# Two of the four value products of the token mixer, their sums and the experts' preparation start in the next loop body

## The reference

```python
x = x + tanh(g_xattn[0]) * attention(layernorm(x), ctx, mask)      # 16 heads of 64, causal
# the token mixer: attention among the 16 heads of one token
h = rmsnorm(layernorm(x), gamma1)
q = (h @ Wq + bq).reshape(b, t, 16, 16)
kv = ((h @ Wdown + bdown) @ Wup + bup)                             # k, v: (b, t, 16, 16)
att = softmax(einsum('bthd,btgd->bthg', q, k) / 4)
o = einsum('bthg,btgd->bthd', att, v)
y = layernorm(x) + o @ Wo + bo
# eight experts, all of them weighted by a softmax gate
h2 = rmsnorm(y, gamma2)
gate = softmax(h2 @ Wg + bg)
x = x + tanh(g_ffn[0]) * (y + sum_e gate[e] * (h2 @ We[e]))
```

## Time and profile before

| what | value |
|---|---|
| median of 3 runs | 2502.35 us (2502.28 to 2506.46) |
| the profiled execution's own time | 2502.84 us |
| its span, first to last instruction | 2501.0 us |
| mean granted PE clock over the span | 0.961 |
| PE busy | 2227.4 us (89%) |
| DVE busy | 1480.4 us (59%) |
| ACT busy | 1267.7 us (51%) |
| POOL busy | 1023.1 us (41%) |

### The profile page before, as it was taken

How to read it: one execution, slowest core, us unless ns; L and a number is a source line. 1 busy time by engine, 2 the same in 40 slices (tenths; PEclk the granted TensorE clock), 3 DMA queues, 4 the chain that set the end, 5 groups by cost and what they waited for, 6 DMA issues and landing times.

```text
span 2501.0 us, 47888 instructions
## 1 busy us (share of the span) xinstructions
PE 2227.4 (89%) x16000; PEld 1887.5 (75%) x16000; DVE 1480.4 (59%) x3922; ACT 1267.7 (51%) x3969; POOL 1023.1 (41%) x907
## 2 busy tenths in 40 slices
PE   5888899898888888888875799999999999999998
PEld 4667677777777777777664688888888888888888
DVE  4466666767667676676767635555555555555551
ACT  5655655556555565555633434455544444445541
POOL 1255555565555655556446213333332322333320
PEclk9999999999999999999977799999999999999999
DMA  4000000000000000000110200000000000000000
GB/s 154 8 12 14 6 17 17 17 13 4 17 17 17 13 4 17 17 17 4 39 32 13 110 16 7 13 17 17 17 17 17 17 17 16 5 13 17 17 9 9
DMA packets 26000, 51.40 MB, mean 21 GB/s; under 512 B 6160, under 2 KB 7312, under 8 KB 24784
## 3 DMA queue, kind: packets, MB, share of 16 engines
q1 hardware_dynamic: 25936, 50.57, 6.0%
HBM read 42.17 MB, written 8.39 MB: 20 GB/s over the span
## 4 chain that ended last, share of the span: by engine, by line
PE 57%; DVE 15%; ACT 8%; POOL 6%; issue 6%; DVEq 4%; POOLq 2%; DMA 0%; ACTq 0%
PE l_ffn L1714 13%; POOL l_prod L385 5%; PE l_ffn L161 4%; PE l_attn L161 4%; PE l_ffn L162 4%; PE l_ffn L163 4%; PE l_attn L1675 4%; PE l_attn L163 3%; PE l_attn L162 3%; DVEq L735 3%; PE l_side L161 3%; PE l_heads L1689 2%; POOLq L355 2%; PE l_side L163 2%; PE l_side L162 2%
## 5 line engine op out<-in xcount | busy, mean ns | idle before, releaser
L1253 POOL TENSOR_SCALAR l_probs<-l_probs,l_rinv 128x256 f32<-128x256 f32 x512 | 240.3, 484 | 479.2 <-DVE l_rinv L1492 478.3
L1376 ACT ACTIVATE l_probs<-l_score,l_negmax 128x256 f32<-128x256 f32 x512 | 239.1, 474 | 268.2 <-DVE l_negmax L1487 268.1
L385 POOL TENSOR_TENSOR l_prod<-l_att,l_kv 128x2048 f32<-128x2048 f32 x64 | 288.5, 4542 | 164.6 <-DVE l_att L672 164.6
L371 POOL TENSOR_TENSOR l_prod<-l_q,l_kv 128x2048 f32<-128x2048 f32 x64 | 291.2, 4561 | 150.7 <-DVE l_att L655 86.6
L1714 PE MATMUL l_ffn<-l_w,l_hid 128*128 128x256 f32 x1536 | 348.6, 381 | 1.0 <-ACT l_hid L1337 1.0
L1714 PEld LDWEIGHTS l_ffn<-l_w,l_hid 128*128 128x128 f32 x1536 | 286.2, 190 | 48.8 <-issue 12.7
L1499 DVE COPY l_probsT<-l_attn 128x512 f32<-128x512 f32 x240 | 164.5, 686 | 142.8 <-PE l_attn L1675 142.8
L745 DVE CUSTOM_DVE_ANT_0 l_probs<-l_score,l_mbias 128x256 f32<-128x256 f32 (+1 forms) x512 | 161.3, 352 | 144.9 <-PE l_score L947 95.8
L678 DVE TENSOR_REDUCE l_h<-l_prod 128x128 f32<-128x2048 f32 x64 | 146.3, 2286 | 107.5 <-POOL l_prod L385 107.2
L468 ACT ACTIVATE l_probs<-l_probs,l_negmax 128x256 f32<-128x256 f32 x256 | 130.8, 511 | 107.7 <-DVE l_negmax L745 106.6
L1487 DVE TENSOR_REDUCE l_negmax<-l_score 128x2 f32<-128x512 f32 x256 | 175.0, 684 | 15.0 <-PE l_score L1663 13.7
(11 more groups left out here) (261 smaller groups left out, 7177.2 us busy)
## 6 DMA issues: line engine op xcount, KB each, us to landing
l_ctxin<-in_ctx SPq DMA_DIRECT2D x32, 256.0 KB, 3.0
l_xin<-in_x SPq DMA_DIRECT2D x16, 256.0 KB, 2.6
l_x<-in_x SPq DMA_DIRECT2D x16, 256.0 KB, 2.6
x<-l_acc SPq DMA_DIRECT2D x16, 256.0 KB, 2.0
l_xin<-x SPq DMA_DIRECT2D x16, 256.0 KB, 3.1
l_x<-x SPq DMA_DIRECT2D x16, 256.0 KB, 2.6
out<-l_x SPq DMA_DIRECT2D x16, 256.0 KB, 2.0
l_hid<-in_w SPq DMA_DIRECT2D x2, 1536.0 KB, 8.2
```

Source lines behind the costliest of these rows:

```text
L371: nc.gpsimd.tensor_tensor(prod[:, u].rearrange("p (h g d) -> p h g d", h=half, g=H), q4[:, u * half:(u + 1) * half].unsqueeze(2).to_broadc ...
L385: nc.gpsimd.tensor_tensor(prod[:, u].rearrange("p (h d g) -> p h d g", h=half, d=HD), a4.unsqueeze(2).to_broadcast([P, half, HD, H]), v4.u ...
L1253: last = nc.gpsimd.tensor_scalar(probs[:, j % 4, t * S:(t + 1) * S], probs[:, j % 4, t * S:(t + 1) * S], rinv[:, j, t:t + 1], 1.0, ALU.mul ...
L1376: last = nc.scalar.activation(probs[:, s % 4, t * S:(t + 1) * S], ps[:, t * S:(t + 1) * S], ACT.Exp, bias=negmax[:, s, t:t + 1], accum_out ...
```

## The change

In the first layer, two of the four `weigh` products (pieces 2 and 3), with their sums, are issued in the following body. The transposition and output product of `o` move from the start of a body to steps 3 and 4, the residual sum to step 4, the squares to 5, the scaling to 6, `h2T` to step 7, the gate to step 8, and the experts' products from steps 6 to 17 to steps 9 to 18. The mixer's own matmuls move one step back, and so does the preparation of the next batch. POOL makes the mask of the next batch at the end of a body instead of this batch's at its beginning. Buffers change with it: `o` lies in `y` and no longer in `h`, its transpose in `h2T`; `n` and `x1` are copied to `nres` and `x1res` at step 9; the normalised input is written over the input (`xn = xin`), so that the next load of `x` waits for its transpose.

```diff
-    xin, ctxin, xn = sb(left, "xin", [P, NT, D]), sb(left, "ctxin", [P, ND, S]), sb(left, "xn", [P, NT, D])
+    xin, ctxin = sb(left, "xin", [P, NT, D]), sb(left, "ctxin", [P, ND, S])
...
-    oT = qT
+    xn, oT = xin, qT
...
-    o, foT = h, hT
+    o, foT = y, h2T
...
-    mix_at = {2: "hT", 3: "q", 4: "down", 5: "up0", 6: "up1"}
-    expert_at = {6: 0, 7: 1, 8: 2, 10: 3, 12: 4, 14: 5, 15: 6, 17: 7}
-    add_at = {7: 0, 8: 1, 9: 2, 10: 3, 12: 4, 14: 5, 15: 6, 17: 7}
-    score_at = {7: 0, 9: 1, 11: 2, 12: 3}
-
-    gather_at = {15: 0, 16: 1, 18: 2, 19: 3}
+    mix_at = {3: "hT", 4: "q", 5: "down", 6: "up0", 7: "up1"}
+    moe_at = {3: "oT", 4: "out", 7: "h2T", 8: "gate"}
+    expert_at = {9: 0, 10: 1, 11: 2, 13: 3, 14: 4, 16: 5, 17: 6, 18: 7}
+    add_at = {10: 0, 11: 1, 12: 2, 14: 3, 15: 4, 17: 5, 18: 6, 19: 7}
+    score_at = {8: 0, 9: 1, 11: 2, 12: 3}
+
+    gather_at = {16: 0, 18: 1}
...
         def load(b):
             if not first(b):
-                sp.wait_ge(xn_ready, b)
+                sp.wait_ge(xT_hi, b)
...
         def body(a, b, c, nxt):
             yield BEGIN
-            if a is not None:
-                mask(a)
+            if c is not None:
+                weigh(c, 2)
             if b is not None:
                 power(varB_ready, rstdB_ready, varB, rstdB, b)
-            if b is not None:
                 power(ms1_ready, r1_ready, ms1, r1, b)
+            yield 0.5
             if c is not None:
-                power(ms2_ready, r2_ready, ms2, r2, c)
+                weigh(c, 3)
+            yield 3.2
             if nxt is not None:
                 split_context(nxt)
                 power(varA_ready, rstdA_ready, varA, rstdA, nxt)
+            yield 5.2
+            if c is not None:
+                power(ms2_ready, r2_ready, ms2, r2, c)
...
-                for piece in range(4):
-                    yield 13.5 + piece
-                    weigh(b, piece)
+                yield 13.8
+                weigh(b, 0)
+                yield 15
+                weigh(b, 1)
+            yield 15.9
+            if nxt is not None:
+                mask(nxt)
...
-            if s == 0 and b is not None:
+            if s == 1 and b is not None:
                 mix_rms(b)
-            if s == 1:
-                if c is not None:
-                    moe_squares(c)
-                if b is not None:
-                    V.tensor_copy(x1res[:], x1[:]).then_inc(x1_copied, 1)
+            if s == 2 and c is not None:
+                mix_gather(c, 3)
...
+            if s == 9 and b is not None:
+                V.tensor_copy(nres[:], n[:])
+                V.tensor_copy(x1res[:], x1[:]).then_inc(x1_copied, 1)
...
             yield BEGIN
-            if c is not None:
-                low(side, "oT", c, foT, foT_hi)
             if b is not None:
                 dve.drain()
                 variance(x1, statB, mvB, varB, varB_ready)
             yield BEGIN_OUT
             if c is not None:
-                moe_residual(c)
+                mix_gather(c, 2)
             if b is not None:
                 mix_normalise(b)
...
-            if c is not None:
-                pe.wait_ge(gathered, 4 * (c + 1))
-                transpose4(side, "oT", c, o)
             if a is not None:
                 attn.emptied(pe, "xT", a)
                 project("q0", a)
                 project("q1", a)
             yield BEGIN_OUT
-            if c is not None:
-                side.emptied(pe, "oT", c)
-                tokens(side, "out", c, foT, fo, D)
```

More of the change, by code:

```diff
@@ L200, in layer0 @@
     x1, ytmp = sb(right, "x1", [P, NT, D]), sb(right, "ytmp", [P, NT, D])
-    x1res, n, h = sb(right, "x1res", [P, NT, D]), sb(right, "n", [P, NT, D]), sb(right, "h", [P, NT, D])
+    x1res, nres, n, h = sb(right, "x1res", [P, NT, D]), sb(right, "nres", [P, NT, D]), sb(right, "n", [P, NT, D]), sb(right, "h", [P, NT, D])
     statB, mvB, varB, rstdB = sb(right, "statB", [P, NT, 6]), sb(right, "mvB", [P, NT, 2]), sb(right, "varB", [P, NT]), sb(right, "rstdB", [P, NT])
@@ L231, in layer0 @@
     side = SideBanks(nc, right, both, "l0_side", mix_uses, moe_uses,
-                     ["oT", "out", "hT", "q", "down", "h2T", "up0", "gate", "up1"] + [f"we{j}" for j in range(E)] + ["idle"])
+                     ["hT", "oT", "q", "out", "down", "up0", "up1", "h2T", "gate"] + [f"we{j}" for j in range(E)] + ["idle"])
     raw_in, split_hi, split_lo = [sem("raw_in0"), sem("raw_in1")], sem("split_hi"), sem("split_lo")
@@ L314, in sync @@
         load_residual(B - 1)
-        yield 17
+        yield 19.6
         store(B - 3)
@@ L401, in body @@
                 power(varA_ready, rstdA_ready, varA, rstdA, nxt)
+            yield 5.2
+            if c is not None:
+                power(ms2_ready, r2_ready, ms2, r2, c)
             if b is not None:
-                yield 5.5
+                yield 6.5
                 query_key(b, 0, 0)
-                yield 6.5
+                yield 7.5
                 query_key(b, 0, 1)
-                yield 8.5
+                yield 8.8
                 query_key(b, 1, 0)
-                yield 9.5
+                yield 10
                 query_key(b, 1, 1)
-                for piece in range(4):
-                    yield 13.5 + piece
-                    weigh(b, piece)
+                yield 13.8
[5 more added lines that the diff above has]
+                mask(nxt)
         split_context(0)
         power(varA_ready, rstdA_ready, varA, rstdA, 0)
+        mask(0)
         run(body(0, None, None, 1))
@@ L506, in before_exp @@
                 nc.scalar.activation(dT[0][:], ps[0:LAT, 0:S], ACT.Identity, bias=bdown[:]).then_inc(dT_hi, 1)
-            if c is not None and s == 4:
+            if c is not None and moe_at.get(s) == "oT":
+                high(side, "oT", c, foT[0], foT_hi)
+            if c is not None and moe_at.get(s) == "h2T":
                 high(side, "h2T", c, h2T[0], h2T_hi, gamma2)
         def beside_head(a, b, c, nxt, s):
-            if c is not None and s == 5:
+            if c is not None and s == 8:
                 act.wait_ge(glog_ready, c + 1)
@@ L516, in beside_head @@
                 last.then_inc(gexp_done, 1)
-            if c is not None and s == 6:
+            if c is not None and s == 9:
                 act.wait_ge(gsum_ready, c + 1)
@@ L537, in body @@
             yield BEGIN
-            if c is not None:
-                high(side, "oT", c, foT[0], foT_hi)
             if a is not None:
@@ L687, in moe_residual @@
             dve.drain()
-            V.tensor_tensor(y[:], y[:], n[:], ALU.add)
+            V.tensor_tensor(y[:], y[:], nres[:], ALU.add)
             dve.drain()
@@ L783, in beside_head @@
             if c is not None:
-                if s == 2:
+                use = moe_at.get(s)
+                if use == "oT":
+                    low(side, "oT", c, foT, foT_hi)
+                elif use == "out":
+                    moe_residual(c)
+                elif s == 5:
+                    moe_squares(c)
+                elif s == 6:
                     moe_normalise(c)
-                elif s == 4:
+                elif use == "h2T":
                     low(side, "h2T", c, h2T, h2T_hi, gamma2)
-                elif s == 5:
+                elif use == "gate":
                     moe_gate_logits(c)
-                elif s == 6:
+                elif s == 9:
                     moe_gate(c)
@@ L1011, in beside_head @@
             if c is not None:
-                if s == 4:
+                use = moe_at.get(s)
+                if use == "oT":
+                    pe.wait_ge(gathered, 4 * (c + 1))
+                    transpose4(side, "oT", c, o)
+                elif use == "out":
+                    side.emptied(pe, "oT", c)
+                    tokens(side, "out", c, foT, fo, D)
+                elif use == "h2T":
                     pe.wait_ge(h2_ready, c + 1)
                     transpose4(side, "h2T", c, y)
-                elif s == 5:
+                elif use == "gate":
                     side.emptied(pe, "h2T", c)
```

4 lines of the change are left out of this document (2 added, 2 removed).

## The result

The change made the kernel slower: 2661.4 us (median of 4 runs, 2659.0 to 2665.9) against 2504.4 us (4 runs) for the kernel before, a ratio of 1.063 with an interval of 1.061 to 1.065. The forecast was 2478, its range 2447 to 2508. The profiled execution of the changed kernel took 2661.3 us with a span of 2659.5.

What follows compares the result with a forecast made beforehand. PE was nearest its limit, but POOL's `weigh` products were taken to hold the first layer's 78.4 us bodies. From 2502.8, 14 x 1.6 = 22 and 2 at the hand-over gave 2479, as median 2478; range 2447 to 2508 us.

Steps and rivals of the forecast that it cites:

- At no cost: Middle body: two copies at step 9, one new (0.4 us), and SP's loads lie beside other work and cost nothing.
- A body: First layer, from the end of PE's output product to the next: 76.8 us, 1.6 less than 78.4.
- The start on DVE: Start of a body: first row maximum at E + 6.8 instead of E + 9.5, so heads begin 2.7 us earlier.
- The added wait for sum 3: Step 3, PE's transposition of `o` waits 2.1 us for DVE's sum of product 3; bounds zero and 6.8.
- slower: Rival, chance 0.14: the in-order wait at sum 3 becomes the bound, PE's losses pass 11.3 us a body; 2523 us.
- h2T and the experts: Middle of a body: `h2T` waits 1.7 us in step 7 for scaled `y`; third expert waits 1.2 us for an addition.
- The wait for `xT_lo` and the low clock behind it: Later in a body: PE's 2.48 us wait for the next batch's `xT` low part and the low clock both go.
- the clock takes it back: Rival, chance 0.14: the clock falls in the thin new start, 1.6 us per body are lost again; 2500 us.
- The hand-over: Passage to the second layer: two of POOL's last four products move behind L1253; 2 us gained, bounds 5 lost, 9 gained.
- The sum: Whole kernel: 2502.8 less 22 for 14 bodies and 2 for the hand-over gives 2479, as median 2478 us.
- the likeliest case: The forecast itself, chance 0.52: 2478 us, reaching from 2466 to 2492.

Runs made afterwards that it cites:

- a7: Changed kernel with the scalings of `h`, `y` and the next input in accumulating form and the two copies as reductions: 2490.8 us, ratio 0.996.
- b4: Kernel before with its four sums of weighed values at steps 16, 17, 18, 19 in place of 15, 16, 18, 19: 2533.4 us, ratio 1.013.
- b5: Kernel before with its four sums at steps 16 to 19 and 21 constant-weight matmuls ahead of the transposition of `o`: 2504.0 us, ratio 1.000.
- a12: Changed kernel with constant-weight matmuls in PE's waits, 16 ahead of the transposition of `o` and 42 ahead of that of `y`: 2625.7 us, ratio 1.049.
- a11: Changed kernel with three scalings accumulating, two copies as reductions, and the hand-over's POOL products 2 and 3 ahead of the power of `varF`: 2483.7 us, ratio 0.993.
- a1: Changed kernel with the scalings of `h` and `y` in accumulating form and the two copies as reductions: 2559.4 us, ratio 1.022.
- a9: Changed kernel with three scalings (`h`, `y`, next input) accumulating, two copies as reductions, and the second layer's `xf` accumulating too: 2491.7 us, ratio 0.996.
- b3: Kernel before with one added DVE `tensor_tensor` (n + n, read by nobody) at step 8, beside a POOL q*k product: 2568.5 us, ratio 1.027.
- a3: Changed kernel with only the scaling of `y` in accumulating form: 2628.1 us, ratio 1.050.

## Why the prediction was wrong

The step that failed is the one headed "At no cost", and with it every term in which an instruction of DVE kept its old duration. "Two copies at step 9, one of them new (0.4 us)" took 4.33 + 0.41 us; the scalings of `h` and `y`, which have no term of their own, took 4.08 and 4.82 instead of 0.61 and 1.01. I asked of each instruction what it would wait for in the queues and what lay beside it on PE, and never what POOL would be doing at that moment. Moving product 3 to E + 7.4 put it exactly over the scaling of `h`.

- *A body:* forecast 76.8, measured 88.7. With the stalls taken out (a7) 76.8. Of the 11.9 us between the two, PE's idle time has 6.8 (88.7 - 72.9 against 76.8 - 67.8, means of the bodies shown) and its longer matmuls 5.1. The 78.4 us of a body before were read rightly, but not as far as 1166.55: from 614.84 that is seven bodies and 3 us more, for one body there took 81.4.
- *The start on DVE:* forecast first maximum at E + 6.8; E is 702.04, where PE has ended the output product, and the maximum stands at 708.73, E + 6.7. Product 3 was to run from E + 7.4: 709.27 is E + 7.2.
- *The added wait for sum 3:* forecast 2.1, measured 2.1 (a7 2.2). The rival "slower" put its trouble there. Its sign came true and its place did not: this wait never grew.
- *h2T and the experts:* forecast 1.7 and 1.2, measured 5.4 and 3.3 (13.3 / 4); in a7 1.5 and 1.3.
- *The wait for `xT_lo` and the low clock behind it:* both gone from that place in a7, as forecast. But it fell at two other places, in about every second body each; the mean clock stayed at 0.98, that of before. The sum had put low clock behind the new waits at nothing. The rival "the clock takes it back" had the right mechanism and, in those bodies, the right place, behind step 3, but bodies came down to 76.8 all the same. In the changed kernel PE's matmuls took 5.1 us a body longer than in a7, in b4 3.0 longer than before. With PE at work in those waits the same kernels ran 29 and 36 us faster (b5, a12). The rule of the Trainium skill that the prediction weighed there (TensorE: Matmul & The Clock Gate, "HAM oscillation — how this bites in real kernels") has every such stretch start slow; the waits of 2.8 us in b4 agree with it in 9 of 11 bodies, those of 2.2 us in a7 in 5 of 11.
- *The hand-over:* forecast 2 us gained, bounds 5 lost and 9 gained. Measured without the other stalls (a7) 16 us lost, outside the bounds: 7 of them the stall of `xf`, by a11 (2490.8 - 2483.7), the rest open.
- *The sum:* with the five forms and the hand-over in order the change gives 2483.7, 6 us over the forecast, inside the likeliest case's range. Part of that is luck: in a11 the last `x1` comes 29 us earlier than before (1238.2 against 1267.2) where 22 were forecast, and what follows loses 9 where 2 were to be gained. The queues of a middle body were counted rightly; what two engines share was not.

## What to carry to other kernels

When an instruction of DVE or POOL is moved, ask what the other of the two is doing at that time. Plain copies and scalings between SBUF tensors, and DVE instructions with two SBUF inputs, stood still here until POOL's long instruction was over; the accumulating `tensor_scalar` and `tensor_reduce` didn't, and cost 0.2 to 0.3 us more. When one such stall is mended, look at the next plain instruction behind it: it inherits the product (L611 in a1, L1465 in a9), so it is better to move the long product into idle time (a11). And a wait of PE that grows can have two prices, its length and the clock behind it: look at both before calling a small wait harmless.

## What the runs showed of the hardware

- A DVE copy of 128x512 beside a POOL product of 4.6 us took 3.5 to 4.4 us in place of 0.42, a `tensor_tensor` of that size with both inputs in SBUF 3.7 to 4.7 in place of 0.69 (b3), and a `tensor_scalar` of only 128x2 4.3 in place of 0.17 (L608 in a11, L602 in a7). POOL's products were not lengthened by it: 4.47 to 4.61 us in the kernel before, 4.46 to 4.66 in the changed one.
- The stall can outlast one product. In a3 one copy (L809, at 1333.06) began 1 us ahead of the end of a product, and took 5.80 us, until the product behind that one was over too (1334.01 to 1338.57).
- The same work as a `tensor_reduce` over an axis of one element took 0.66 to 0.69 us beside the product, and a `tensor_scalar` of 128x256 that also writes its sum 0.47 us plus 0.08 us to read the accumulator, against 0.35 for the plain form.
- 58 matmuls of no use in a body made the changed kernel 1.3% faster (a12): they filled waits behind which the clock otherwise stood at 0.50. PE's waits of 2.2 us in a7 had that clock behind them in 5 of 11 bodies, those of 2.8 us in b4 in 9 of 11, those of 1.5 us for the last sum in the kernel before in none.
